# A three-stage software pipeline moved one slot deeper: parameters in a ring of their own, state matmuls ahead of the transposes, the out-projection three slots behind

## The reference

```
h      = x * rsqrt(mean(x*x) + EPS) * norm_w
proj   = einsum('bsd,od->bso', h, in_proj_w)       # gate 8192, hidden 8192, B 1024, C 1024, dt 128
hid, B, C = silu(causal_conv(hidden|B|C, conv_w, conv_b))      # 4 taps
dt     = softplus(dt + dt_bias);  A = -exp(A_log)
M      = (C @ B.T) * exp(segsum(A * dt))           # 128 heads of 64 channels, 8 groups share B and C
y      = M @ (hid * dt) + Dp * hid
yg     = y * silu(gate)
ygr    = yg * rsqrt(mean over each group's 1024 channels of yg*yg + EPS)
out    = x + einsum('bsd,od->bso', ygr * gnorm_w, out_proj_w)
```

## Time and profile before

| | |
|---|---|
| median of 3 runs | 825.29 us (823.76 to 825.86) |
| profiled execution, its own time | 823.68 us |
| its span, first to last instruction | 821.9 us |
| mean granted clock of TensorE | 0.992 |
| TensorE busy | 790.5 us, 96% of the span |
| VectorE, ScalarE, GpSimd busy | 612.4, 603.8, 615.7 us |

### The profile page before, as it was taken

The page is one execution under the profiler, slowest core; times in us unless marked ns, Lnnn a source line. Parts: engine busy times, 40 slices in busy tenths (PEclk is TensorE's granted clock), DMA queues, the critical chain, the costliest instruction groups (busy, mean ns, idle before and its releaser), DMA issues.

```text
span 821.9 us, 13293 instructions
## 1 busy us (share of the span) xinstructions
PE 790.5 (96%) x4319; PEld 610.7 (74%) x4322; DVE 612.4 (75%) x752; ACT 603.8 (73%) x1052; POOL 615.7 (75%) x552
## 2 busy tenths in 40 slices
PE   8799899999999999999999999999999999989897
PEld 7567677777777777777777777777777777767664
DVE  6768987777786867776786867776786867787774
ACT  5778786888688876878688886878688886877442
POOL 6669966799578986799578986799578985795231
PEclk9999999999999999999999999999999999999999
DMA  8433324334234324333233314334233324340001
GB/s 332 148 92 127 129 65 155 128 120 138 90 128 128 128 64 154 128 128 128 90 128 128 128 64 154 128 128 128 90 128 128 128 65 155 128 154 1 4 2 52
DMA packets 48812, 94.93 MB, mean 116 GB/s; under 512 B 3952, under 2 KB 36848, under 8 KB 48784
## 3 DMA queue, kind: packets, MB, share of 16 engines
q1 hardware_dynamic: 48496, 94.06, 34.6%
q10 hardware_dynamic: 288, 0.52, 0.2%
HBM read 93.26 MB, written 1.31 MB: 115 GB/s over the span
## 4 chain that ended last, share of the span: by engine, by line
PE 62%; DVE 17%; ACT 11%; issue 7%; DMA 0%; POOL 0%; ACTq 0%; DVEq 0%
PE ps_z L1093 19%; PE ps_out L1196 15%; PE ps_h L1093 13%; PE ps_y L1183 7%; DVE conv_bc L728 4%; DVE conv L728 4%; ACT decay L531 4%; PE ps_t L1066 2%; ACT L531 2%; ACT conv L477 2%; DVE v L846 2%; DVE yg L852 2%; DVE decay L786 2%; ACT conv_bc L461 1%; DVE y_lo L858 1%
## 5 line engine op out<-in xcount | busy, mean ns | idle before, releaser
L728 DVE SCALAR_TENSOR_TENSOR conv<-ps_h,w_raw,conv 128x510 f32<-128x510 f32 (+2 forms) x192 | 143.2, 746 | 102.1 <-ACT conv L477 97.6
L531 ACT ACTIVATE decay<-csx,cs_own 128x256 f32<-128x256 f32 (+1 forms) x512 | 184.4, 443 | 1.0
L297 POOL TENSOR_TENSOR win_lo<-w_raw,win_hi 128x1024 fp32r<-128x1024 f32 x64 | 153.1, 2392 | 0.9 <-DMA csx<-cs_rows 0.9
L399 POOL TENSOR_TENSOR sqacc<-sqacc,sq 128x512 f32<-128x512 f32 x47 | 69.8, 1486 | 107.1 <-ACT sq L567 107.1
L786 DVE TENSOR_TENSOR decay<-decay,cbm 128x1536 f32<-128x1536 f32 x64 | 126.0, 1969 | 3.6 <-ACT decay L531 3.6
L1183 PE MATMUL ps_y<-decay,hid_dt 128*64 128x256 f32 (+1 forms) x1024 | 98.9, 336 | 16.1 <-DVE hid_dt L835 16.1
L539 ACT ACTIVATE hidT<-conv 128x512 f32<-128x512 f32 x64 | 40.5, 633 | 100.5 <-DVE conv L728 100.5
L1183 PEld LDWEIGHTS ps_y<-decay,hid_dt 128*64 128x64 f32 x1024 | 64.1, 138 | 58.9 <-DVE hid_dt L835 21.8
L337 POOL TENSOR_SCALAR_AFFINE_SELECT csx<-csx 128x512 f32<-128x512 f32 x128 | 102.1, 823 | 0.5 <-DMA csx<-cs_rows 0.5
L1196 PE MATMUL ps_out<-wout_hi,y_lo 128*128 128x512 f32 x252 | 99.9, 396 | 0.0
L1196 PE MATMUL ps_out<-wout_hi,y_hi 128*128 128x512 f32 x252 | 99.5, 395 | 0.0
(11 more groups left out here) (314 smaller groups left out, 1514.2 us busy)
## 6 DMA issues: line engine op xcount, KB each, us to landing
w_raw<-in_wmain SPq DMA_DIRECT2D x64, 772.0 KB, 4.3
csx<-cs_rows SPq DMA_DIRECT2D x128, 256.0 KB, 3.5
bc_raw<-in_wbc SPq DMA_DIRECT2D x8, 517.0 KB, 3.5
ctx_raw<-in_ctx SPq DMA_DIRECT2D x1, 2048.0 KB, 16.2
bc_raw<-in_wffn SPq DMA_DIRECT2D x2, 512.0 KB, 3.8
out_x<-acc SPq DMA_DIRECT2D x4, 256.0 KB, 2.1
acc<-in_x ACTq DMA_DIRECT2D x2, 256.0 KB, 3.9
acc<-in_x SPq DMA_DIRECT2D x2, 256.0 KB, 3.7
```

What stands on the lines that cost most here:

```text
L297: eng.tensor_tensor(win_lo[:, r2, :], w_raw[:, r4, 0:W_IN], win_hi[:, r2, :].bitcast(f32), ALU.subtract).then_inc(low_win, 1)
L399: eng.tensor_tensor(sqacc[:], sqacc[:], sq[:, (k - 1) % 2, :], ALU.add).then_inc(pool_sq, 1)
L531: done = eng.activation(decay[:, r2, b, h, lo:lo + n], csx[:, r2, b, h, lo:lo + n], ACT.Exp, bias=cs_own[:, r2, t, h:h + 1])
L728: eng.scalar_tensor_tensor(out=out_b[:, :, back:], in0=src_b[:, :, 0:S - back], scalar=w[:, TAPS - 1 - back:TAPS - back], in1=out_b[:, :, ...
```

## The change

1. The 8 parameter columns leave `w_raw`. They get a tile `par` of one column block for each pair of a group and a DMA of their own for each pair (128 rows of 32 bytes). The load of `w_raw` now waits on `low_wout` (GpSimd has split the old content) and no longer on `dve_ylo`.
2. TensorE's slot: h(s), z(s), out(s-3), scan(s-1), tr(s), and for k = 0 and 7 h, out, z, scan, tr. The products of B and C stand after z, in `ps_h` and `ps_t`.
3. VectorE: `combine` works on pair s-2 and stands first in the slot, then `scale_hidden`, the mask (of pair s-1, function `mask`), `conv_hidden`, `lower_y` (pair s-2). `add_group` and `mean_squares` come one slot later.
4. ScalarE: `decays(s)` first in slot s, then `tap`, `finish_y` (pair s-2), `hidden`, `gates`.
5. GpSimd waits on `pe_gate` (z of the pair before) ahead of a slot's splits where it waited on `pe_out`; the split of the out-projection is done at the end of the slot, for pair s.
6. Three buffers in `sq`; two more out-projections and one more `combine`, `finish_y` and `lower_y` after the last slot.

The core of the diff:

```
             for r in range(4):
+                eng.dma_start(par[:, r, :], wpar_d[r]).then_inc(w_in[r], 16)
                 eng.dma_start(w_raw[:, r, :], wmain_d[r]).then_inc(w_in[r], 16)
...
+                    if late(s - 7):
+                        eng.wait_ge(dve_ylo, s - 7)
+                    eng.dma_start(par[:, k, :], wpar_d[s]).then_inc(w_in[r], 16)
                     if late(s - 3):
-                        eng.wait_ge(dve_ylo, s - 3)
+                        eng.wait_ge(low_wout, s - 3)
                     eng.dma_start(w_raw[:, r, :], wmain_d[s]).then_inc(w_in[r], 16)
...
                 if not (last and k == PPG - 1):
-                    eng.wait_ge(w_in[n4], 16 * (2 * g + (k + 1) // 4 + 1))
-                    if first and 0 < k < 3:
+                    eng.wait_ge(w_in[n4], 32 * (2 * g + (k + 1) // 4 + 1))
+                    if late(s):
                         eng.wait_ge(pe_gate, s)
-                    if late(s - 2):
-                        eng.wait_ge(pe_out, s - 2)
...
                 if not (last and k == PPG - 1):
                     split_in(n4, (k + 1) % 2)
-                    split_out(n4)
                     eng.wait_ge(csx_in[1 - r2], 32 * (4 * g + (k + 1) // 2 + 1))
                     lower_in(n4, (k + 1) % 2, s + 2)
                     select(1 - r2)
-                    lower_out(n4, s + 2)
+                if late(s - 3):
+                    eng.wait_ge(pe_out, s - 3)
+                if k == 3 and not first:
+                    eng.wait_ge(dve_ms, g)
+                    eng.tensor_tensor(rstd[:], ms[:], half_neg[:], ALU.pow).then_inc(pool_rstd, 1)
+                sum_squares(s, g, k, first)
+                split_out(r4)
+                lower_out(r4, s + 1)
...
             # scalar, slot
+                decays(s, k)
+                if k == PPG - 1 and not last:
+                    tap_bc(0, g + 1, ps_z, conv_bc[:])
                 if k == 0:
                     tap_bc(1, g, ps_z, conv_bc[:])
-                    silu_bc(1, g, conv_bc[:])
...
+                tap(s, g, k)
                 finish_y(s, g, k, first)
-                if not (last and k == PPG - 1):
-                    decays(s + 1, k + 1)
...
+                hidden(s, k)
+                gates(s, k)
...
             # vector, slot
+                if not (first and k < 2):
+                    combine(s, k)
                 if not (first and k == 0):
                     scale_hidden(s, k)
-                if k == 2 and not first:
+                if k == 3 and not first:
                     add_group(g - 1)
+                if not (first and k == 0):
+                    mask(s, g, k)
...
+                conv_hidden(s, k)
+                if not (first and k < 2):
+                    lower_y(s, k)
...
             # tensor, slot
+                turned = k == 0 or k == PPG - 1 and not last
...
                 project(ps_h[:], win_hi[:, r2, 0:KT * P], win_lo[:, r2, 0:KT * P], pe_hid)
                 if first and k == 0:
                     start_up()
+                if turned and not (first and k == 0):
+                    project_out(s, g, k)
...
+                project(ps_z[:], win_hi[:, r2, KT * P:], win_lo[:, r2, KT * P:], pe_gate)
+                if not turned and not (first and k < 3):
+                    project_out(s, g, k)
+                if k == 0:
+                    products_of_bc(s, g)
+                if k == 2 and not first:
+                    sum_channels(s, g - 1)
                 if not (first and k == 0):
                     scan_heads(s, k)
...
             slots(eng, slot)
+            project_out(PAIRS, GROUPS, 0)
             scan_heads(PAIRS, 0)
-            project_out(PAIRS, GROUPS, 0)
+            eng.wait_ge(low_wout, PAIRS - 1)
+            project_out(PAIRS + 1, GROUPS, 1)
```

More of the change, by code:

```diff
@@ L19 @@
 N_PAR = 8
-W_ROW = W_ALL + N_PAR
 BC_W = 2 * KT * P
@@ L63, in build @@
         cs_tok = sb("cs_tok", [P, TT, HEADS])
-        w_raw = sb("w_raw", [P, 4, W_ROW])
+        w_raw = sb("w_raw", [P, 4, W_ALL])
+        par = sb("par", [P, PPG, N_PAR])
         win_hi = sb("win_hi", [P, 2, W_IN], f32r)
@@ L482, in _ @@
             tap_bc(0, 0, ps_z, conv_bc[:])
+            tap(0, 0, 0)
             tap_bc(1, 0, ps_y, gate[:, 1, :])
-            tap(0, 0, 0)
             silu_bc(0, 0, conv_bc[:])
@@ L519, in slot @@
                     scale_context(PPG - 1)
+                if k == PPG - 1 and not last:
+                    silu_bc(0, g + 1, conv_bc[:])
+                if k == 0:
+                    silu_bc(1, g, conv_bc[:])
+                hidden(s, k)
+                gates(s, k)
             def decays(s, k):
@@ L555, in finish_y @@
             def finish_y(s, g, k, first):
-                q2, q4 = (k - 1) % 2, (k - 1) % 4
-                eng.wait_ge(dve_yg, s)
-                if late(s - 2):
-                    eng.wait_ge(pe_out, s - 2)
+                q2 = k % 2
+                eng.wait_ge(dve_yg, s - 1)
+                if late(s - 3):
+                    eng.wait_ge(pe_out, s - 3)
                 eng.activation(y_hi[:, q2, :], yg[:, q2, :], ACT.Copy,
-                               scale=w_raw[:, q4, W_ALL + 6:W_ALL + 7]).then_inc(act_yhi, 1)
-                if not (first and k < 3):
-                    gs, ks = (g, k - 3) if k >= 3 else (g - 1, k - 3 + PPG)
-                    eng.wait_ge(pool_sq, (PPG - 1) * gs + max(ks, 1))
-                eng.activation(sq[:, q2, :], yg[:, q2, :], ACT.Square).then_inc(act_sq, 1)
+                               scale=par[:, (k - 2) % PPG, 6:7]).then_inc(act_yhi, 1)
+                if not (first and k < 5):
+                    gs, ks = (g, max(k - 4, 0)) if k >= 3 else (g - 1, k - 4 + PPG)
+                    eng.wait_ge(pool_sq, (PPG - 1) * gs + ks)
+                eng.activation(sq[:, 2 if k == 2 else q2, :], yg[:, q2, :], ACT.Square).then_inc(act_sq, 1)
             slots(eng, slot)
@@ L793, in slot, with mask @@
                     quantise_context(k - 2)
+                if first and k == PPG - 1:
+                    eng.wait_ge(pre_pool, POOL_RSTD + TT)
                 if last and k in (4, 5):
                     quantise_context(k + 2)
+            def mask(s, g, k):
+                eng.wait_ge(act_exp, s)
+                if k == 1:
+                    eng.wait_ge(dve_cb, 2 * g + 2)
+                q2 = (k - 1) % 2
+                eng.tensor_tensor(decay[:, q2], decay[:, q2], cbm[:].unsqueeze(2).broadcast_to([P, B, 2, MJ]),
+                                  ALU.mult).then_inc(dve_m, 1)
             def conv_hidden(s, k):
                 eng.wait_ge(act_tap, s + 1)
-                convolve(conv[:], ps_h[:], w_raw[:, k % 4, W_ALL:W_ALL + TAPS], dve_conv, 3 * s)
+                convolve(conv[:], ps_h[:], par[:, k, 0:TAPS], dve_conv, 3 * s)
             def constants():
@@ L879, in _ @@
             slots(eng, slot)
+            mask(PAIRS, GROUPS, 0)
+            combine(PAIRS, 0)
             scale_hidden(PAIRS, 0)
-            combine(PAIRS, 0)
             lower_y(PAIRS, 0)
+            combine(PAIRS + 1, 1)
+            lower_y(PAIRS + 1, 1)
             eng.wait_ge(ffn_split, 1)
@@ L1159, in slot @@
                     eng.wait_ge(dve_cb, 2 * g + 2)
-                if k == 1 and not first:
+                if k == 2 and not first:
                     eng.wait_ge(dve_ms, g)
@@ L1171, in slot, with products_of_bc @@
                             wbc_lo[:, which * KT * P:(which + 1) * KT * P], pe_bc)
+            def products_of_bc(s, g):
+                eng.wait_ge(act_bc, 2 * g + 2)
+                eng.wait_ge(dve_conv, 3 * s + 3)
+                if late(s):
+                    eng.wait_ge(dve_hiddt, s)
+                for b, bank in ((1, ps_h), (0, ps_t)):
+                    q = b * S
+                    mm(bank[:, 0:S], bcT[:, 0, q:q + P], bcT[:, 1, q:q + S], start=True, stop=True)
+                    mm(bank[:, S:MJ], bcT[:, 0, q + P:q + S], bcT[:, 1, q + P:q + S], start=True,
+                       stop=True).then_inc(pe_cb, 1)
             def scan_heads(s, k):
@@ L1188, in project_out @@
             def project_out(s, g, k):
-                pair, q2, q4 = (k - 2) % PPG, (k - 2) % 2, (k - 2) % 4
-                eng.wait_ge(dve_ylo, s - 1)
+                pair, q2, q4 = (k - 3) % PPG, (k - 3) % 2, (k - 3) % 4
+                eng.wait_ge(dve_ylo, s - 2)
                 for t in range(TT):
-                    if k == 2 and late(TT * g):
+                    if k == 3 and late(TT * g):
                         eng.wait_ge(dve_acc, TT * (g - 1) + t + 1)
```

156 lines of the change are left out of this document (63 added, 93 removed).

## The result

The changed kernel takes 839.59 us (median of 4 runs, against 825.54 for the kernel before on the same chip): ratio 1.016, interval 1.012 to 1.020. One of the four runs (961.55 us) was disturbed and is left out of the ratio; the median of the other three is 838.61. So it is slower by 13 us. The profiled execution took 838.61 us with a span of 836.6. I had forecast 807, so the prediction was wrong, and on the wrong side of no change.

A forecast was written before the change was run, and what follows sets the result against it. TensorE's own work bounds middle groups; elsewhere it idles mostly before scans, waiting for hid_dt. Gains of 18.1 us less 1.5 for k = 3 net 16.6, from 823.68 to 807 us; range 803 to 812, with near rivals 798 to 818.

The forecast's parts named there:

- Parameters and loads: SyncE's 64 more DMAs and w_raw's load: no cost while issued over six us ahead, else at most 3.5 us once.
- The scan: TensorE's scan starts at 8.6 us in the slot, the mask is ready at 3.7; all gaps ahead of scans go.
- The transposes, the start: Transposes have two us left, one in group 0; at the start two waits of 2.2 us, gain 1.3.
- k = 3: Slot with add_group before the mask: hidden at 9.5 still meets transposes at 10.05; charged 0.2 us a group, 1.5 in all.
- Middle groups: Wait in k = 4 of each middle group goes: 0.39 us times 6, gain 2.3 us.
- switches: TensorE's changes between matmul kinds: one surplus dropped, one gained; 0.04 us for each of 60 slots, gain 2.4 us.
- k = 0 and 7: Slots with out ahead of z: z starts at 5.8 us, conv of B or C ends about 4.3; nothing waits.
- Group 7 and the tail: Group 7 gains 4.4 us less 0.3 from a wait and slow rows; the tail gains 0.8 at the last scan.
- The slow one: Rival: chain from scan to transposes grows too long in every slot, at 0.6 us a slot 843 us; chance 0.05.
- No wait left: Rival: the switch between matmul kinds costs nothing and no wait remains, 801.6 us; chance 0.13.
- the rival of k = 3: Rival: the chain to the transposes is late in k = 3 or more, 1.5 us a group, 816 us; chance 0.17.
- The rule of the shared port pair: VectorE and GpSimd block each other for whole instructions; the mask could wait, costing TensorE 1.6 us in k = 3.

The follow-up runs named there:

- a_bc2: The changed kernel with one edit: SyncE issues the load of B's and C's weights in slot k = 2, not k = 1; 806.92 us, ratio 0.977.
- a_rstd_scan: a_bc2_rstd with the scan put back between h and what follows, the deeper pipeline kept; 876.33 us, ratio 1.063.
- a_bc2_rstd: a_bc2 with GpSimd's rstd of slot k = 3 ahead of the causal mask of csx instead of behind it; 799.53 us, ratio 0.969.

## Why the prediction was wrong, step by step

**The step that failed** is "Parameters and loads": "`w_raw` for a slot is issued more than six us ahead of its split. Cost nothing while that lead holds; without it, at most the landing time of 3.5 us once, at the start." In all slots but one the load is issued ten us or more ahead of the split. For the split in k = 1 GpSimd asks (308.55) before the load is even issued (311.26). In k = 1 the queue has a load that waits on `act_bc`, and I had listed silu of C only as "long done" for TensorE's products; I never asked who else waits for it. `a_bc2` shows the price: 33 us, from 3.2 to 6.1 us in each of groups 1 to 6 (5.4 in group 3, 95.99 for 90.59), not 3.5 once. The bound was wrong too, because I took a late load to cost what is missing of its landing, where it puts GpSimd back by 5 us and TensorE pays for that with a wait of 2.4 and half clock behind it, or with a second chain of waits in k = 3. In k = 2 of group 3: gap 2.54 for 0, sums 1.80 for 0.87, scan 2.75 for 1.45, transposes 0.77 for 0.42, together 5.1 of the 16.20 - 11.09. The first of each pair is by starts in the rows of the changed kernel above, the second by those of `a_bc2` in k = 2:

```profile
325.03 0.39 PE L1220 MATMUL ps_out<-wout_hi,y_lo 128*128 128x512 f32 x1
325.26 0.95 PE L1229 MATMUL ps_t<-ones,sqacc 128*128 128x1 f32 x8
326.13 1.52 PE L1207 MATMUL ps_y<-decay,hid_dt 128*64 128x256 f32 x16
327.58 0.66 PE L1083 MATMUL ps_t<-ident,hidT 128*128 128x128 f32 x4
328.00 1.18 PE L1110 MATMUL ps_h<-hT_hi,win_hi 128*128 128x512 f32 x4
```

The other steps are judged in `a_bc2`, the changed kernel without that fault: forecast 807.1, profiled 805.3, median 806.9. (The sum has a slip: with group 7 at 4.4 less 0.3 the gains add up to 17.8 and not to 18.1, which gives 807.4.) That the total is near is in part luck, as the terms show: the middle groups gained more than forecast, and the clock fell twice where the forecast had it up.

- *The scan.* Right: no wait ahead of a scan over 0.6 us in `a_bc2`. `a_rstd_scan` shows that the deeper pipeline by itself does not free it; with its old place it waits again.
- *The transposes, the start.* Two waits of 2.12 and 1.53 for the forecast 2.2 and 2.2. But the clock did not hold: soon after the first wait h runs at 1.2 GHz (four of its matmuls, at 43.84, take 1.91 us for 1.07), and the granted clock is 0.67 from 42 to 46 us and 0.90 from 46 to 50, which is 1.7 us lost. So the forecast that the two waits cost nothing beyond themselves failed, within the bound of 2.8 that stood beside it. Start and group 0 together: h of k = 1 in group 1 stands at 134.77 before and at 123.48 in `a_bc2`; less the out-projection of 2.8 that is deferred, 8.5 us gained. Forecast 1.3 + 6.9 = 8.2.
- *k = 3.* The mechanism was right, `rstd` late and `add_group` behind it; 0.2 us a group was too little. TensorE waited 0.3 to 1.3 us in each, and an earlier `rstd` gave 4.9 us.
- *Middle groups.* Six of them gain (687.66 - 134.77) - (669.68 - 123.48) = 6.7 us, forecast some 3 (2.3, less k = 3, and the switches). The term that was too small is **switches**: 0.04 us a slot. A quiet slot is 10.45 before, 10.41 in `a_rstd_scan` and 10.31 in `a_bc2_rstd`. These last two differ in the place of the scan alone, so the switch is worth 0.10; the other 0.04 is the place in SBUF, which the forecast did not have.
- *k = 0 and 7.* Nothing waits, 0.2 us once ahead of z.
- *Group 7 and the tail.* 134.24 us before and 133.62 in `a_bc2`, with the deferred out-projection 3.4 gained; forecast 4.1 and 0.8, 4.9 together. Up to the first matmul of the cross product the gain is 5.0 (91.31 before, 89.13, and 2.8); behind it `a_bc2` loses 1.6 (44.49 for 42.93), by the clock: 0.92 granted from 758.8 to 780 us, where the kernel before has 1.00.
- *The rivals.* The slow one (843) came near the measured time by a chain that did not occur: no exponential or conv was slow. "No wait left" (801.6) is not what `a_bc2` does; `a_bc2_rstd` comes near it (799.5), with the waits of the start still there. For the rival of k = 3 (816) the wait is there, but at 0.3 to 1.3 us a group and through `rstd`, not through the mask, which takes 1.75 us in k = 3 of groups 2 to 7.
- *The rule of the shared port pair* ("SBUF — State Buffer", section "SBUF: two separate sides", in the Trainium skill) was weighed for the mask. It bears on both sides. VectorE's mask in `a_bc2`, which takes 1.75 us in the earlier trace rows and here 2.17, as in the median of all 64:

```profile
318.91 2.17 DVE L808 TENSOR_TENSOR decay<-decay,cbm 128x1536 f32<-128x1536 f32 x1
```

And GpSimd's rows beside it:

```profile
317.79 1.68 POOL L339 TENSOR_SCALAR_AFFINE_SELECT csx<-csx 128x512 f32<-128x512 f32 x2
319.44 2.79 POOL L403 TENSOR_TENSOR sqacc<-sqacc,sq 128x512 f32<-128x512 f32 x1
```

The sum of squares, 1.26 us where it runs alone, starts beside the mask and ends 1.15 after it: as if it had stood still until the mask was done. The mask itself starts beside `select`, which ends at 319.47, and is 0.42 us longer than in the earlier trace rows. By that rule, the trace agrees. The mask has that time to spare. GpSimd has not: it runs without a gap from 303.72 to 332.85, and the `rstd` that `add_group` waits for in k = 3 is made in that stretch, at 329.86. So these meetings may be part of the wait of k = 3; no run isolates them.
